# A 12-layer decoder on one core: one meeting between parts, one block per element in the last state-space layer, attention maxima by half elements, first stacks on two queues

## The reference, cut to what matters

```python
# layer 1 attention: 16 heads of 16, causal; layer 2: 32 heads of 8, rotary;
# layer 3 cross attention: 32 heads of 8, keys and values from a context
out = softmax(q @ k.T * scale) @ v
x = x + out @ Wo + bo
# layer 3 mixer, a state-space layer of 32 heads of 64, per element:
z, xs, B, C, a = split(x @ W_in)            # 2048 columns each, a: 32
decay = cumsum(-exp(a))                     # per head over tokens
y = (tril(exp(decay_t - decay_s)) * (C @ B.T)) @ xs + D * xs
x = x + norm(y * silu(z)) @ W_out           # norm over the 2048, gamma and beta folded in
```

## Time and profile before

| what | us |
|---|---|
| median of 3 runs (2307.3 to 2311.36) | 2310.94 |
| the profiled execution | 2317.7 |
| its span, first to last instruction | 2315.9 |
| PE, DVE, ACT, POOL busy | 1925.9, 1746.4, 1370.6, 556.9 |
| first, second, third attention with their projections | about 124, 190, 203 |
| last state-space layer, four elements | about 465 |
| mean granted TensorE clock, share of full speed | 0.861 |

### The profile page before, as it was taken

One profiled execution on the slowest core, in us unless ns is written; L12 is line 12 of the kernel. 1 busy time (PEld: TensorE's weight loads), 2 busy tenths in 40 slices (PEclk: granted clock), 3 DMA queues, 4 the chain that ended last, 5 costly groups with the idle time before them and its releaser, 6 DMA issues. The chain is left out here.

```text
span 2315.9 us, 34034 instructions
## 1 busy us (share of the span) xinstructions
PE 1925.9 (83%) x10675; PEld 1279.2 (55%) x10675; DVE 1746.4 (75%) x3955; ACT 1370.6 (59%) x2782; POOL 556.9 (24%) x775
## 2 busy tenths in 40 slices
PE   6999999967777776876867985699999999869888
PEld 4767677754433433643653543466767676634545
DVE  6999899968999998747987855576555555679734
ACT  5888888857999996355434565424343535354641
POOL 3766677712111101004621001100111111120000
PEclk9999999987677676885777897699999999977999
DMA  8222222203121102304303000152111111052010
GB/s 299 84 84 87 90 82 89 83 2 112 54 61 55 48 1 88 103 10 96 52 19 94 22 3 19 53 210 74 38 36 37 36 37 37 1 134 66 13 38 19
DMA packets 85187, 148.54 MB, mean 64 GB/s; under 512 B 11439, under 2 KB 61055, under 8 KB 82571
## 3 DMA queue, kind: packets, MB, share of 16 engines
q1 hardware_dynamic: 81760, 141.86, 19.4%
q0 software_dynamic: 1728, 4.22, 0.8%
q10 hardware_dynamic: 1536, 0.49, 0.1%
HBM read 135.03 MB, written 11.01 MB: 63 GB/s over the span
## 5 line engine op out<-in xcount | busy, mean ns | idle before, releaser
L1309 DVE SCALAR_TENSOR_TENSOR moe_acc<-moee_eo,moe_wsel,moe_acc 128x256 f32<-128x256 bf16 x512 | 208.0, 477 | 4.3 <-ACT moee_eo L1221 4.1
L1208 PE MATMUL moee_po<-moee_db,moee_hb 96*128 96x256 bf16 (+1 forms) x768 | 146.9, 366 | 42.8 <-ACT moee_eo L1221 38.7
L926 POOL TENSOR_SCALAR l_dec<-l_cumR,l_cum 128x128 f32<-128x128 f32 x192 | 160.9, 848 | 2.8 <-DMA l_ec<-l_rows 2.8
L951 DVE SCALAR_TENSOR_TENSOR l_acc<-l_px,l0w_chan,l_acc 128x253 f32<-128x253 f32 (+2 forms) x288 | 136.2, 473 | 29.4 <-POOL l_acc L906 27.9
L1208 PEld LDWEIGHTS moee_po<-moee_db,moee_hb 96*128 96x128 bf16 (+1 forms) x768 | 97.4, 129 | 98.9 <-ACT moee_eo L1221 44.8
L1221 ACT CAST moee_eo<-moee_po 128x512 bf16<-128x512 f32 x256 | 131.7, 592 | 11.3 <-PE moee_po L1208 10.5
L1758 ACT ACTIVATE l3xa_ex<-l3xa_pS 128x512 f32<-128x512 f32 x128 | 74.4, 604 | 79.1 <-PE l3xa_pS L1667 78.6
L1758 ACT ACTIVATE l2a_ex<-l2a_pS 128x512 f32<-128x512 f32 x128 | 74.1, 605 | 75.5 <-PE l2a_pS L1667 75.0
L596 PE MATMUL l_pz<-xT,l0w_w_in 128*128 128x256 f32 x388 | 113.3, 416 | 0.0
L3193 POOL TENSOR_TENSOR l3w_yz<-l3b_ys,l3b_sz 128x256 f32<-128x256 f32 x48 | 40.2, 838 | 281.7 <-DVE l3b_ys L3234 281.7
L1167 POOL CAST moee_wb<-moe_wf 128x512 bf16<-128x512 f32 x48 | 29.9, 623 | 310.9 <-DVE moee_hb L1325 247.5
(11 more groups left out here) (597 smaller groups left out, 5345.8 us busy)
## 6 DMA issues: line engine op xcount, KB each, us to landing
l_cumR<-l_rows SPq DMA_DIRECT2D x48, 512.0 KB, 3.5
l3w_cumR<-l_rows SPq DMA_DIRECT2D x32, 512.0 KB, 3.6
l_ec<-l_rows SPq DMA_DIRECT2D x96, 128.0 KB, 3.8
moe_wf<-in_moe_up SPq DMA_DIRECT2D x48, 256.0 KB, 2.6
l3w_w_in<-in_l_w_in SPq DMA_DIRECT2D x1, 8224.0 KB, 26.6
m1b_bc<-bc_rows SPq DMA_DIRECT2D x16, 512.0 KB, 6.1
moe_df<-in_moe_down SPq DMA_DIRECT2D x48, 128.0 KB, 2.6
l_qs<-parts_q SPq DMA_DIRECT2D x36, 128.0 KB
```

What stands on the lines that cost most here:

```text
L926: last = nc.gpsimd.tensor_scalar(dec[:, u % 2, e, S:SC], cumR[:, slot, 2 * (u % CU) + e, P:S], cum[:, b % 2, 1, head:head + 1], 0.0, ALU.a ...
L951: nc.vector.scalar_tensor_tensor(out=a, in0=px[:, u % 2, 0:S - (L0_CONV - 1 - c)], scalar=w, in1=a, op0=ALU.mult, op1=ALU.add).then_inc(ta ...
L1208: last = nc.tensor.matmul(po[:, t, :], hb[rows, j % H, t * P:(t + 1) * P], db[rows, j % H, :], start=(n == 0), stop=(n == len(parts) - 1))
L1309: last = nc.vector.scalar_tensor_tensor(out=acc[:, t, :], in0=eo[:, e % 2, t, :], scalar=wsel[:, t, e:e + 1], in1=acc[:, t, :], op0=ALU.mu ...
```

## The change

1. `Stage` no longer uses blocks and barriers. Each engine's program is written straight on; on leaving a part each engine drains, adds one to `arrived` and waits until all five have; POOL then clears the part's semaphores and adds one to `cleared`, which the other four engines await at the end of the next part. Parts use two alternating ranges of semaphores. A `Stage` without a program has no meeting. The part inside the loop keeps one barrier.
2. `mamba3_heads` and `mamba3_ends` become `mamba3_element`, one part per element. The copy of the next input stands on POOL ahead of its last product; PE goes from the last outputs to the decay columns and four of the eight projections, then does the output projection, then the other four. The accumulators share eight banks.
3. In `attend` the maxima are taken by half elements (H/2 heads): eight transpositions, copies and triples of row DMAs instead of four; DVE keeps the copy, POOL does the five splitting operations; the lag is H/2 + 13 steps; the output transposition and projection come two steps later.
4. In `project_heads` SP stores only the first half of the tokens, then loads the key stack of element 0 itself; POOL loads the query stack as soon as its pieces are out. The stores of the second half stand on SP in `attend`, ahead of the loads of element 2; ACT loads the query stack of element 1.

```diff
-SEM_BASE = 110
+SEM_BASE = (106, 162)
+SEM_ARRIVED = 218
...
+    def leave(self):
+
+        nc, arrived, cleared = self.nc, Stage.arrived, Stage.cleared
+        for engine in (nc.tensor, nc.vector, nc.scalar, nc.sync):
+            if Stage.passed:
+                engine.wait_ge(cleared, Stage.passed)
+        Stage.passed += 1
+        for engine in (nc.tensor, nc.vector, nc.scalar, nc.gpsimd, nc.sync):
+            engine.drain().then_inc(arrived, 1)
+        for engine in (nc.tensor, nc.vector, nc.scalar, nc.gpsimd, nc.sync):
+            engine.wait_ge(arrived, 5 * Stage.passed)
+        if self.sems:
+            nc.gpsimd.sem_clear(range(self.base, self.base + len(self.sems)))
+        nc.gpsimd.sem_inc(cleared, 1)
...
                                ).then_inc(first_in, 16)
-                for n in range(PIECES):
-                    sends = len(range(n, len(items), PIECES))
-                    if sends:
-                        pool.wait_ge(sent[n], 32 * sends)
+                for n in range(KT):
+                    pool.wait_ge(sent[n], 32)
                 load_rows(pool, stacks[0], 0, qparts, 0, 0, HD, first_in)
-                load_rows(pool, stacks[1], 0, kparts, 1, 0, HD, first_in)
...
+                for u in range(len(items)):
                     sp.wait_ge(split_done, u + 1)
-                    for e in range(2):
-                        sp.dma_start(out[:, 2 * half + e, :, :].rearrange("n w t -> w n t"),
-                                     parts[0:width, u % PIECES, :, e * S:(e + 1) * S]
-                                     ).then_inc(sent[u % PIECES], 16)
-
-
-def carry(nc, st, name, at, units):
-
-    sems = [nc.alloc_semaphore(f"{name}_{n}", num=SEM_CARRIED + (PIECES + 1) * at + i)
-            for i, n in enumerate(("sent0", "sent1", "sent2", "sent3", "first_in"))]
+                    send_pieces(sp, carried, u, units[u])
+                sp.wait_ge(cleared, 2)
+                for n in range(KT, len(items)):
+                    sp.wait_ge(sent[n], 32)
+                load_rows(sp, stacks[1], 0, kparts, 1, 0, HD, carried["first_k"])
...
     N = B * H
-    LAG = H + 12
-    AHEAD = 1 if H > 16 else 2
+    HH, W = H // 2, 2 * B
+    LAG = HH + 13
     OUT_AT, TURN_AT, NORM_AT = 5, 8, 9
-    MAX_AT, ROWS_AT, O_AT, PROJ_AT, ADD_AT = 1, 7, H + 6, H + 7, H + 8
...
+                units = carried["units"]
                 for u in range(1, RING):
                     if u == 2:
+                        for late in range(len(units) // 2, len(units)):
+                            send_pieces(sp, carried, late, units[late])
                         for n in range(PIECES):
-                            sp.wait_ge(carried["sent"][n], 32 * len(range(n, carried["units"], PIECES)))
+                            sp.wait_ge(carried["sent"][n], 32 * len(range(n, len(units), PIECES)))
                     load_rows(sp, ks, u, kparts, 1, u, HD, k_in[u])
-                    load_rows(sp, qs, u, qparts, 0, u, HD, q_in[u])
                     sp.dma_start(ks[KR:KR + 3, u, :, :], g["in"]["ones_rows2"][:, 0:NKV, :]).then_inc(k_in[u], 16)
+                    if u >= 2:
...
+                def split_max(w):
+                    now, rest, parts = mT[:, w % 2, :], mrest[:, w % 2, :], mparts[:, w % 2, :, :]
+                    if w >= 2:
+                        pool.wait_ge(m_rows[w - 2], 16 * 3)
+                    pool.wait_ge(m_taken, w + 1)
+                    nc.gpsimd.tensor_copy(parts[:, 0, :], now).then_inc(m_part, 1)
+                    pool.wait_ge(m_part, 4 * w + 1)
+                    nc.gpsimd.tensor_tensor(rest, now, parts[:, 0, :], ALU.subtract).then_inc(m_part, 1)
+                    pool.wait_ge(m_part, 4 * w + 2)
+                    nc.gpsimd.tensor_copy(parts[:, 1, :], rest).then_inc(m_part, 1)
+                    pool.wait_ge(m_part, 4 * w + 3)
+                    nc.gpsimd.tensor_tensor(rest, rest, parts[:, 1, :], ALU.subtract).then_inc(m_part, 1)
+                    pool.wait_ge(m_part, 4 * w + 4)
+                    nc.gpsimd.tensor_copy(parts[:, 2, :], rest).then_inc(m_split, 1)
+
+                nc.gpsimd.memset(vb[:, :, :, :, HD + 1:], 0.0)
...
+                def turn_max(w):
+                    u, heads = w // 2, slice(w % 2 * HH, (w % 2 + 1) * HH)
+                    pe.wait_ge(maxed, (w + 1) * HH)
+                    if added_by(w):
+                        pe.wait_ge(added, added_by(w))
                     for t in range(ST):
-                        last = nc.tensor.transpose(pE[0:H, t * P:(t + 1) * P], negm[:, u % 2, t, :], ident[:, :])
+                        last = nc.tensor.transpose(pE[0:HH, t * P:(t + 1) * P], negm[:, u % 2, t, heads], ident[:, :])
                     last.then_inc(m_turned, 1)
...
+                load_rows(act, qs, 1, qparts, 0, 1, HD, q_in[1])
...
+        mamba3_element(nc, g, "l3s", m, None, 0)
         with nc.Fori(0, B - 1) as b:
-            mamba3_heads(nc, g, "l3b", m)
-            mamba3_ends(nc, g, "l3c", m, b, b + 1)
-        mamba3_heads(nc, g, "l3h", m)
-        mamba3_ends(nc, g, "l3e", m, B - 1, None)
+            mamba3_element(nc, g, "l3b", m, b, b + 1)
+        mamba3_element(nc, g, "l3e", m, B - 1, None)
 
...
+                if heads:
+                    for j in range(L3_J):
+                        if j == L3_J - 1 and start is not None:
+                            pool.wait_ge(z_done, L3_J)
+                            nc.gpsimd.tensor_copy(xin[:, :, :], xT[:, :, start, :]).then_inc(x_in, 1)
+                        pool.wait_ge(ys_done, j + 1)
+                        nc.gpsimd.tensor_tensor(yz[:, j, :], ys[:, j % 2, :], sz[:, j % 2, :],
+                                                ALU.mult).then_inc(yz_done, 1)
+                else:
...
+                    outputs(L3_J - 1)
+                if start is not None:
+                    pe.wait_ge(x_in, 1)
+                    if heads:
+                        pe.wait_ge(xd_done, L3_J)
+                    for k in range(KT):
+                        last = nc.tensor.matmul(pa[0:L3_H, 0:S], w_in[:, k, AC:AC + L3_H], xin[:, k, :],
+                                                start=(k == 0), stop=(k == KT - 1))
+                    last.then_inc(a_proj, 1)
+                    for n in range(FIRST_X):
+                        project(n)
+                if heads:
+                    pe.wait_ge(yz_done, L3_J)
+                    pe.wait_ge(sz_done, L3_J)
+                    pe.wait_ge(bc_done, L3_J)
+                    for t in range(ST):
+                        cols = slice(t * P, (t + 1) * P)
+                        for j in range(L3_J):
+                            nc.tensor.matmul(po[:, t, 0:D + 1], yz[:, j, cols], w_out[:, j, :],
+                                             start=(j == 0), stop=(j == L3_J - 1))
+                        if t == 0:
+                            pe.wait_ge(summed, L3_J)
+                            pe.wait_ge(ys_done, L3_J)
+                        nc.tensor.matmul(pq[:, t:t + 1], squares[:, cols], g["ones"][:, 0:1],
+                                         start=True, stop=True).then_inc(used, 1)
+                if start is not None:
+                    for n in range(FIRST_X, NX):
+                        project(n)
...
+                if start is not None:
+                    act.wait_ge(a_proj, 1)
+                    nc.scalar.activation(al[:, 0, :], pa[0:L3_H, 0:S], ACT.Exp).then_inc(a_exp, 1)
+                    if heads:
+                        nc.scalar.preload_act_table_set(EXP_LN)
+                        act.wait_ge(masked, L3_J)
+                        act.wait_ge(y_done, L3_J)
+                    for n in range(NX):
+                        if n == ROOT and heads:
+                            root()
+                        take(n)
+                else:
```

More of the change, by code:

```diff
@@ L1356, in load_rows, with send_pieces @@
         ).then_inc(done, 16)
+def send_pieces(queue, carried, u, unit):
+    (w, ws, bias, tables, src, out), half = unit
+    for e in range(2):
+        queue.dma_start(out[:, 2 * half + e, :, :].rearrange("n w t -> w n t"),
+                        carried["pieces"][0:w.shape[2], u % PIECES, :, e * S:(e + 1) * S]
+                        ).then_inc(carried["sent"][u % PIECES], 16)
 def project_heads(nc, g, name, items, v, stacks, qparts, kparts, HD, carried, tables_of=()):
     units = [(item, half) for half in range(2) for item in items]
+    carried["units"] = units
     steps = range(max(len(units), NT))
@@ L1608, in batch_at, with half_at, scores_of, added_by @@
             return u if (j - lag) % H == 0 and 0 <= u < B else None
+        def half_at(i, lag):
+            w = (i - lag) // HH
+            return w if (i - lag) % HH == 0 and 0 <= w < W else None
+        def scores_of(at):
+            u, n = at // H, at % H
+            half, t, pair = n // HH, n % HH // (HH // 2), n % (HH // 2)
+            return u, t, half * (HH // 2) + pair
+        def added_by(w):
```

(23 more changed lines are left out.)

532 lines of the change are left out of this document (249 added, 283 removed).

## The result

The changed kernel takes 2243.38 us (median of 4 runs, 2239.09 to 2246.68), the kernel before on the same chip 2309.12 (2305.8 to 2311.36): a ratio of 0.9707, 95% interval 0.9691 to 0.9723, 65.7 us less. The forecast was 2237 in a range of 2221 to 2263. Between the two profiled executions the step is 2317.7 to 2242.82, 74.9 us; the sum of the prediction was 74.4. Against the medians that sum is 8.7 us too large, and that it meets the step between the two profiles is luck: one of its parts gave far less than forecast, and stages that it did not count gave as much more.

The account below looks back on a forecast made before the run. No engine is busy throughout (PE 83%, DVE 75%); time lies in hand-overs as much as work. Savings of 19.5, 22.7, 18 and 14.2 sum to 74.4 us: profiled 2317.7 becomes 2243.3, less 6.8 for the median, 2237; range 2221 to 2263.

Parts of the forecast that it names:

- Part 1, meetings: Boundaries between program parts: drains and a shared count replace barriers, saving 19.5 us (bounds 17.9 and 22.2).
- the meeting at 0.25 us: At each part boundary: the new meeting taken at 0.25 us, between bounds of 0.15 and 0.31.
- Rival 3: Part boundaries: the meeting costs what the barriers cost, 0.6 us each, saving only 5 us; 2251 us, chance 0.08.
- Part 2, one block per element: Last state-space layer: PE's wait filled and its clock kept, saving 22.7 us (bounds 15 and 23.5).
- Part 3, halves: Three attentions: maxima by half elements shorten the lag to exponentials, saving 18 us (bounds 0 and 24).
- a half costs one transposition and one copy, I take 0.7: Middle of the second attention: each half element adds 0.7 us, where a whole element's split cost 1.1 to 1.4.
- The first stretches: Attention starts, before exponentials: second attention 31.5 to 20.5 us, third alike, first attention 21.2 to 14.6.
- rival 1: Attention pays nothing: halves cost 1.4 us each, rows land late, the saved steps are given back; 2255 us, chance 0.22.
- That DVE holds up POOL's split: Attention: DVE may slow the splitting operations on POOL by a tenth.
- rival 4: Attention: ACT waits for POOL's chain per half element, making the kernel slower, 2338 us at 1.8 us per operation; chance 0.03.
- Part 4, first stacks on two queues: Projection ends: POOL and SP share the twelve stack loads, so POOL's drain stops holding the meeting; 14.2 us (bounds 9 and 15).
- Rival 2: First stacks: key stack lands after DVE's end or third element's stacks late, halving that saving; 2244 us, chance 0.12.

Follow-up runs that it names:

- undo_meeting: The changed kernel with every stage's old exit again (block barrier, then a semaphore-clearing barrier; containers close with their own): 2266.37 us, ratio 0.9795.
- rows_by_sync: The changed kernel with SP issuing each half element's three row DMAs after POOL's split, ACT keeping only the first half's: 2229.83 us, ratio 0.9653.
- unrolled: The changed kernel with the three middle elements of the third state-space layer written out instead of looped: 2245.07 us.
- undo_halves_queues: The changed kernel with attention by whole elements and the first stacks and stores as before, both at once: 2268.96 us, ratio 0.9833.

## Why the prediction came out right, and which parts of it were not

**The last line.** The number on record, 2237, is 6.4 us below the median and inside the range. The sum of 74.4 us met the 74.9 between the two profiled executions, but the change is worth 65.7 by the medians (64.0 to 71.4). The profiled execution of before was a slow one: executions of that kernel scatter over 2301 to 2321, and its mixture of experts, which no edit touches, took 365.3 us where the other twelve traces have 360.3 to 364.5. Against the profiles the sum is right by luck, as the last paragraph of this section adds up; against the medians it is 8.7 too large.

**Part 1, meetings: right in kind, undersized.** The step that was mis-sized is the meeting at 0.25 us: where no engine comes late it leaves 0.05 to 0.13, outside the lower bound of 0.15. At 0.07, 16 boundaries give 0.69 each and 11 give 1.17, in all 24.3 instead of 19.5. The whole runs put undo_meeting's loss at 22.4 or, against the kernel before beside it, 17.6, so they can't tell 24.3 from 19.5; the gaps in the traces can. What I didn't count is the clock ahead of the last expert layer: that stage is 0.7 to 4.0 us shorter in the traces with the new meeting. Rival 3 had 0.08 and is refuted by undo_meeting.

**Part 2, one block per element: right.** Every sign came: the wait 0.70 (0.6 forecast), full clock, the four projections in the place, 3.7 us in the last element (3.5), a period of 108.8 (about 110). The layer gave 25.0 us against 22.7; of the surplus 1.3 is what undo_meeting loses in this layer, the rest is open.

**Part 3, halves: the failed part.** The step "a half costs one transposition and one copy, I take 0.7" is wrong in its cause. A half cost 1.0 to 1.2 us, because ACT issues its three row DMAs ahead of the next exponential. The old cost of a whole element had another cause. In the timeline of the kernel before, the group of the earlier trace rows that took 4.56 us runs from 1303.78 to 1308.34; in it PE waits for DVE, which has the split between its reductions, and ACT's issues of that element come only behind it:

```profile
1306.28 0.39 PE L1651 MATMUL l2a_pA<-l_ks,l_qs 96*128 96x256 bf16 x2 [0.45 <-DVE l2a_negm L1789]
...
1310.35 0.53 ACTq L1770 DMA_DIRECT2D l_qs<-l2a_mparts  x1
1310.52 0.61 ACT L1758 ACTIVATE l2a_ex<-l2a_pS 128x512 f32<-128x512 f32 x1
1310.91 1.25 ACTq L1770 DMA_DIRECT2D l_qs<-l2a_mparts  x2
```

There an exponential stood between the first issue and the other two, and the four heads beside the issues took 3.61 us instead of 3.4. So the prediction halved a cost that the move of the split to POOL removed, and had none for the issues, which had cost 0.2 us before. I had written that each row DMA occupies ACT's queue as before, and had twice as many of them, but priced only PE and DVE. In the middle of the second attention the prediction had six halves at 0.7, 4.2 us; seven came, some 7.3 us. In the first attention, where the eight steps of a half take some 7 us, first to last exponential lengthened by 7.0. The second attention's three stretches came to 145.7 us against the forecast 139.3; before, they took 148.6 (the prediction's own 31.5, 78.2 and 38.9, which it adds up to 147.8). So 2.9 us were gained in them, for a forecast of 7.5. The first stretches are right (28 us; 20.5 forecast for the second, 21.9 measured, of which 1.0 is the key stack). So rival 1, at 0.22, was half right: the steps were given back, though not by late rows, PE's waits for which are 1.2 us at most. That DVE holds up POOL's split didn't show either: 0.39 us for a cast and 0.66 for a subtraction, less than the earlier trace rows. ACT waited for the split only at the first half of each attention, where it issues 0.03 us behind it; later the split was done 1.2 to 5.4 us before ACT took it up, so rival 4 was far off.

**Part 4, first stacks on two queues: right.** Projections are 16.0 us shorter, about 13.5 without their meetings (2 x 0.69 + 1.17), for 14.2; DVE ends two of three and SP is 0.2 us behind in the other. The late stacks of the third element in the first attention, 1.6 to 2.1 us, were counted. Rival 2 came true only in small, with 1.0 us for the key stack in the second attention. What I missed is the tie with part 3: without the halves, the stores inside the attention cost the third one 5 to 6 us (164.8 against 159.8 and 158.9).

In all, projections and attentions gave 25.2 us where parts 3 and 4 with their meetings (5.0) had 37.2; the rest of the program gave 49.7 by the profiles where 37.2 were forecast (22.7, and 14.5 of meetings). 12 missing in one place, 12 over in the other: that these cancel is luck. Of the surplus some 3.7 us are the meetings' own (24.3 for 19.5, less the 1.1 that lie in projections and attentions) and up to 4.0 the last expert layer's. The scatter of the one profile of before lies in the rest, and how much it is stays open.

## What to carry to other kernels

When a batch is halved, list what each half issues on every queue, DMA issues included, and ask what stands behind it on that engine: three issues of 0.6 us in ACT's program cost more than the transposition and copy that one looks at. Give the issues to a queue with nothing behind it, and mind its order: what is wanted first has to stand first, loads and small rows alike. A profiled execution is one draw: when an untouched group of matmuls takes 1.99 us in one trace and 3.52 in another, take such differences out of a stage before you lay its length to an edit.

## What the runs showed of the hardware

A meeting by a drain, one shared count and one wait leaves 0.05 to 0.13 us between the last work and the next when no engine comes late; two of the queued barriers leave 0.68 to 0.78 (0.8 to 1.1 in the last state-space layer), three 1.2 to 1.4, and a loop's single barrier with its branch 0.69 to 0.92.

How long PE had rested did not settle the clock that it was then granted. Ahead of the gate matmuls of the last expert layer, it was 1.00 behind a rest of 0.89 us in the changed kernel, 0.75 behind 0.66 in rows_by_sync, 0.71 behind 0.82 in unrolled and 0.61 behind 1.84 in undo_halves_queues; in the last state-space layer it was 1.00 behind 1.64. The last output projection of the second attention took 1.99 us in the kernel before and 3.66 in the changed one, after the same 0.68 us of waiting. What decides it isn't shown here. Such differences of 1.2 to 2.1 us make up much of the scatter between traces.

Three row DMAs occupy the engine that issues them for 1.8 to 2.6 us, and on ACT what stands behind them waits.
